# Second layer of a fused two-layer transformer: which unit each projection and turn is issued in

## What is computed

```python
xn = layernorm(x); x = x + linear_attention(xn) + mixture_of_experts(xn)   # layer 0
xn = layernorm(x); x = x + chunked_attention(xn) + gated_ffn(xn)           # layer 1, changed here

# chunked_attention: 16 heads of 8, scale 8 ** -0.5; a query of a 64-token chunk sees
# all keys up to that chunk's end
probs = softmax(q @ k.T * scale)
energy = probs.sum(-1)            # goes through two steps of a small nonlinear recurrence
probs = probs * (0.5 + 0.5 * gate(energy)); probs = probs / (probs.sum(-1) + 1e-8)
out = (probs @ v) @ W_out.T
# gated_ffn: xr, xk are mixes of each token with the one before it
out = sigmoid(xr @ W_r.T) * (relu(xk @ W_k.T) ** 2 @ W_v.T)
```

## Time and profile before

| | |
|---|---|
| median of 3 runs | 1524.6 us (1523.17 to 1528.86) |
| the profiled execution | 1515.43 us |
| its span, first to last instruction | 1513.5 us |
| PE (TensorE matmul) busy | 1404.1 us, 93% |
| DVE (VectorE) busy | 1177.3 us, 78% |
| ACT (ScalarE) busy | 817.2 us, 54% |
| POOL (GpSimd) busy | 523.3 us, 35% |
| mean granted TensorE clock | 0.984 of 2.4 GHz |

### The profile page before, as it was taken

The page is one execution under the profiler, slowest core; times in us unless marked ns, Lnnn a source line. Parts: engine busy times, 40 slices in busy tenths (PEclk is TensorE's granted clock), DMA queues, the critical chain, the costliest instruction groups (busy, mean ns, idle before and its releaser), DMA issues.

```text
span 1513.5 us, 35393 instructions
## 1 busy us (share of the span) xinstructions
PE 1404.1 (93%) x12926; PEld 904.6 (60%) x12926; DVE 1177.3 (78%) x2687; ACT 817.2 (54%) x1562; POOL 523.3 (35%) x942
## 2 busy tenths in 40 slices
PE   5699999999999899999998999999999999999994
PEld 3467677677776799998884444444444444444432
DVE  4789889889888795456677888888888888888752
ACT  2334534544543333334334677777766777776673
POOL 2333234234233111172312244444434444442121
PEclk8999999999999999999999999999999999999997
DMA  4111111111112566776973444333334443332300
GB/s 119 38 42 52 45 48 44 51 47 44 54 33 66 165 208 209 220 245 208 258 195 62 98 106 105 98 98 102 87 93 102 108 103 97 98 92 70 82 9 14
DMA packets 118205, 151.94 MB, mean 100 GB/s; under 512 B 31269, under 2 KB 83109, under 8 KB 113413
## 3 DMA queue, kind: packets, MB, share of 16 engines
q1 hardware_dynamic: 105160, 119.47, 29.0%
q0 software_dynamic: 12880, 30.30, 6.8%
HBM read 108.35 MB, written 40.83 MB: 99 GB/s over the span
## 4 chain that ended last, share of the span: by engine, by line
PE 48%; DVE 32%; POOL 7%; issue 6%; ACT 5%; DMA 1%; SPq 0%; POOLq 0%; DVEq 0%; ACTq 0%
DVE nmax L1516 8%; PE bank L1948 8%; PE bank L1939 8%; DVE P L1205 7%; PE bank L1816 5%; PE bank L1994 5%; PE bank L2017 4%; ACT P L946 3%; PE bank L1773 3%; PE bank L1850 2%; PE bank L1957 2%; PE bank L1864 2%; DVE t L1080 1%; PE bank L2064 1%; DVE t L1078 1%
## 5 line engine op out<-in xcount | busy, mean ns | idle before, releaser
L1516 DVE TENSOR_REDUCE nmax<-bank 128x1 f32<-128x512 f32 (+3 forms) x704 | 428.8, 634 | 84.6 <-PE bank L1994 83.6
L946 ACT ACTIVATE P<-bank 128x512 f32<-128x512 f32 x640 | 371.2, 599 | 183.2 <-PE bank L2017 178.4
L1994 PE MATMUL bank<-KT,QT 76*128 76x512 bf16 (+3 forms) x1024 | 251.3, 303 | 28.5 <-DVE nmax L1516 20.9
L2017 PE MATMUL bank<-QT,KT 78*128 78x512 bf16 (+3 forms) x1024 | 244.5, 301 | 8.9 <-ACT P L946 5.5
L693 POOL DMA_INDIRECT xs_d<-xn,idx x128 | 124.6, 973 | 306.0 <-PE bank L1773 197.9
L1994 PEld LDWEIGHTS bank<-KT,QT 76*128 76x128 bf16 x1024 | 86.8, 97 | 189.1 <-DVE nmax L1516 130.6
L1816 PE MATMUL bank<-P,V 128*32 128x512 f32 (+3 forms) x2048 | 191.3, 447 | 0.0
L1205 DVE TENSOR_TENSOR P<-bank,early_w 128x512 f32<-128x512 f32 x256 | 158.7, 682 | 41.3 <-PE bank L1773 41.2
L910 ACT ACTIVATE hr<-bank 128x512 f32<-128x512 f32 x142 | 84.8, 597 | 175.0 <-PE bank L1939 172.1
L741 POOL DMA_INDIRECT hT<-ys_d,idx x104 | 103.5, 995 | 159.9 <-PE bank L2017 141.8
L2017 PEld LDWEIGHTS bank<-QT,KT 78*128 78x128 bf16 x1024 | 98.6, 98 | 85.0 <-ACT P L946 31.9
(11 more groups left out here) (257 smaller groups left out, 2228.6 us busy)
## 6 DMA issues: line engine op xcount, KB each, us to landing
QT<-parts_d SPq DMA_DIRECT2D x96, 192.0 KB
P<-in_fc SPq DMA_DIRECT2D x71, 256.0 KB, 2.9
P<-in_proj SPq DMA_DIRECT2D x71, 256.0 KB, 3.2
parts_d<-parts SPq DMA_DIRECT2D x32, 384.0 KB, 2.5
P<-xs_d SPq DMA_DIRECT2D x71, 128.0 KB, 3.0
ys_d<-P POOLq DMA_DIRECT2D x71, 128.0 KB, 3.4
KT<-parts_d SPq DMA_DIRECT2D x64, 128.0 KB
KT<-parts_d SPq DMA_DIRECT2D x32, 192.0 KB
```

Of the source, the lines that this page charges most:

```text
L946: nc.scalar.activation(P[s % 2][:, u, :], bank[k % 2][:, :], ACT.Exp, scale=float(DH) ** -0.5).then_inc(s_sb, 1)
L1516: nc.vector.tensor_reduce(nmax[:, s // TWO, h:h + TWO * nh - 1:TWO, j], max_bank(n, k)[:, 0:nh * w].rearrange("p (h w) -> p h w", h=nh), A ...
L1994: ins = pe.matmul(max_bank(n, k)[:, i * w:(i + 1) * w], QT[n.p][0:MROWS, h, j * 128:(j + 1) * 128], KT[n.p][0:MROWS, h, 0:w], start=True, ...
L2017: ins = pe.matmul(bank[k % 2][:, c:c + n], KT[b.p][0:SROWS, h, 128 * kb:128 * kb + 128], QT[b.p][0:SROWS, h, 128 * kb:T], start=True, stop ...
```

## The change

On TensorE these pieces change their unit, nothing else about them changes:

| piece | before | after |
|---|---|---|
| r projection | (0,1) | (0,2) |
| k projection | (0,2) | (0,4) |
| kv projection | (0,6) | (0,8) |
| value projection of the next sequence | (1,1) | (2,8) |
| second q/k projection | (1,5) | (1,6) |
| first turn of oT | (3,3) | (3,2) |
| turn of y | (3,5) | (3,4) |
| output projection | (3,9) | (3,8) |

ScalarE's readers move with them: tanh of r from before the exponential of (0,3) to that of (0,4), the squares of k from (0,4) to (0,6), the eviction of v from (1,2) to (3,0), the eviction of yT from (3,7) to (3,6). VectorE's gate moves from behind maximum 10 to behind 13, the residual from behind 11 to behind 14. The waits on W5 and W6 follow the new order of the pieces in these banks.

```diff
--- before.py
+++ after.py
@@ -1003,15 +1003,15 @@
                 for s in range(SHEETS):
                     for u in range(UNITS):
                         at = (s, u)
-                        if at == (0, 3) and core:
+                        if at == (0, 4) and core:
                             tanh_r(b)
-                        if at == (0, 4) and core:
+                        if at == (0, 6) and core:
                             square_k(b)
                         if at == (0, 7) and core:
                             shift_high(b, 1)
                         if at == (0, 8) and before_:
                             evac_oT(b + -1, 1)
-                        if at == (1, 2) and after:
+                        if at == (3, 0) and after:
                             evac_v2(b + 1)
                         if at == (2, 8) and core:
                             evac_oT(b, 0)
@@ -1031,7 +1031,7 @@
                             tanh_resp(b + -1)
                         if at in ((3, 2), (3, 4)) and after:
                             scale_before(b + 1, u // 2 - 1)
-                        if at == (3, 7) and before_:
+                        if at == (3, 6) and before_:
                             evac_yT(b + -1, False)
                         if core:
                             exp_scores(b, s, u)
@@ -1627,9 +1627,9 @@
 
                     if m == 9 and core:
                         shift_low(b, 1)
-                    if m == 10 and core:
+                    if m == 13 and core:
                         gate_kv(b)
-                    if m == 11 and core:
+                    if m == 14 and core:
                         gate_residual(b)
                     if m in (2, 3, 4, 5) and front and not b.less(L2 + 1):
                         for c in range(2):
@@ -1952,8 +1952,11 @@
             def q_rows(n, c):
 
                 pe.wait_ge(xnT_sb, n.at(1, 1))
-                if c == 0 and within(n + -1):
-                    pe.wait_ge(v2_sb, n.at(1, -L2))
+                if c == 0 and n.less(L2 + 2):
+                    if within(n + -1):
+                        pe.wait_ge(v2_sb, n.at(1, -L2))
+                elif c == 0:
+                    pe.wait_ge(gated, n.at(1, -1 - L2))
                 pe.matmul(qk_bank(n, c)[:, :], wqkv2[:, c, :], xnT[n.p][:, 1:T + 1], start=True, stop=True).then_inc(qk_ps, 1)
 
             def take_part(n, c, k):
@@ -1964,7 +1967,9 @@
                           skip_group_check=True).then_inc((res_part, low_ps)[k], 1)
 
             def v_rows(n):
-                if within(n + -1):
+                if within(n + -1) and within(n + 1):
+                    pe.wait_ge(*split_read(n + 1, 0))
+                elif within(n + -1):
                     pe.wait_ge(gated, n.at(1, -L2))
                 else:
                     pe.wait_ge(*split_read(n, 0))
@@ -2032,9 +2037,7 @@
 
             def project_out2(n):
                 pe.wait_ge(yT_sb, n.at(1, 1))
-                if within(n + 3):
-                    pe.wait_ge(*split_read(n + 3, 0))
-                elif within(n + 2):
+                if within(n + 2):
                     pe.wait_ge(v2_sb, (n + 2).at(1, 1 - L2))
                 elif within(n + 1):
                     pe.wait_ge(gated, (n + 1).at(1, 1 - L2))
@@ -2047,6 +2050,8 @@
             def k_rows(n):
                 if within(n + -2):
                     pe.wait_ge(out_ready, (n + -1).at(1, -L2))
+                elif within(n + -1):
+                    pe.wait_ge(v2_sb, n.at(1, 1 - L2))
                 else:
                     pe.wait_ge(*split_read(n + 1, 0))
                 pe.wait_ge(blended, n.at(2, 2 - 2 * L2))
@@ -2127,33 +2132,33 @@
                             pv(b + -1, SHEETS - 1, u // 2)
                         if u in (1, 3, 5, 7) and s > 0 and core:
                             pv(b, s - 1, u // 2)
-                        if where == (0, 1) and core:
+                        if where == (0, 2) and core:
                             r_rows(b)
-                        if where == (0, 2) and core:
+                        if where == (0, 4) and core:
                             k_rows(b)
                         if where == (0, 5) and core:
                             turn_max(b, 1)
-                        if where == (0, 6) and core:
+                        if where == (0, 8) and core:
                             kv_rows(b)
                         if where == (1, 0) and before_:
                             turn_oT(b + -1, 1, False)
-                        if where == (1, 1) and after:
+                        if where == (2, 8) and after:
                             v_rows(b + 1)
                         if where == (1, 2) and front:
                             turn_xn(b + 2, False)
-                        if where in ((1, 4), (1, 5)) and front:
-                            q_rows(b + 2, u - 4)
+                        if where in ((1, 4), (1, 6)) and front:
+                            q_rows(b + 2, u // 2 - 2)
                         if where in ((1, 8), (2, 0)) and front:
                             take_part(b + 2, s - 1, 0)
                         if where in ((2, 2), (2, 4)) and front:
                             take_part(b + 2, u // 2 - 1, 1)
                         if where == (2, 6) and after:
                             turn_max(b + 1, 0)
-                        if where == (3, 3) and core:
+                        if where == (3, 2) and core:
                             turn_oT(b, 0, False)
-                        if where == (3, 5) and before_:
+                        if where == (3, 4) and before_:
                             turn_y2(b + -1)
-                        if where == (3, 9) and before_:
+                        if where == (3, 8) and before_:
                             project_out2(b + -1)
 
             over_layer2(pe, body2)
```

## The result

The changed kernel took 1508.9 us in the median of 4 runs (1503.41 to 1512.14), the kernel before 1524.3 us beside it on the same chip. The medians lie 15.5 us apart; by the ratio it is 17.5 us (0.0115 of 1524.3), with its interval 13.3 to 21.8. Forecast were 17.6 us, and 1507 us.

A forecast was written before the change was run, and what follows sets the result against it. Neither TensorE nor VectorE bounds the turn; each waits for the other through two score banks. 1.23 us in 13 turns (16.0) plus 1.8 for edge turns, 17.8, gives 1497.6, scaled to 1507 us; range 1501 to 1516.

The forecast's parts named there:

- right: Signs: period about 42.3 us, no VectorE waits before maxima 3, 14 to 16, new 0.6 before 11, L1560 behind GpSimd.
- wrong: Signs: L1560 directly behind a row maximum with E above 14.6 us; VectorE waits again 6.5 us; ScalarE holding TensorE's scores.
- stretch E: Units (2,1) to (3,4): GpSimd's chain sets L1560, added 1.33 us absorbed in some 1.9 us room; gain 0.
- rival (c): (2,8) to (3,2): v is not absorbed; +0.5 us in 14 turns, 7 to 8 us slower, 1532 us; chance 0.14.
- A: Units (0,0) to (0,4): r behind (0,2)'s scores removes VectorE's 0.73 us wait; bounds 0.4 and 0.8.
- B: Units (0,5) to (0,8): kv moved to (0,8) gives new VectorE idle time of 0.64 us before maximum 11; bounds 0, 0.89.
- C: Units (0,9) to (1,4): v leaves (1,1), gates move in, waits ahead of maxima 14 to 16 go; 1.14 us gained.
- The front's sum: Stretches A, B and C together: 0.73 + 1.14 - 0.64 = 1.23 us gained a turn.
- D: Units (1,5) to (2,0): only the second q moves, from (1,5) to (1,6); TensorE sets it, so unchanged.
- F: Units (3,5) to (3,9): VectorE's 0.56 us wait for the output projection moves one place earlier; 0, bound +0.3.
- Rival (a): Idle times only change place through two banks; 0.3 us a turn stays, 4 us, 1520 us; chance 0.18.
- Rival (b): All VectorE waiting outside D and E goes: 2.4 us a turn, 33 us, 1491 us; chance 0.13.

The follow-up runs named there:

- second measurement: The changed kernel run again with no edit, beside the kernel before: 1500.1 us against 1515.1, ratio 0.9885.
- v alone: Kernel before with only the value projection moved from (1,1) to (2,8), with its eviction and waits: ratio 0.9948 to the kernel before, turn 42.90 us.
- v and the gates: Kernel before with the value projection in (2,8), gate and residual behind maxima 13 and 14, r, k, kv unmoved: ratio 0.9977 to the kernel before.
- v twice: Changed kernel with the value projection in (2,8) computed twice into the same bank: ratio 0.9941 to the kernel before, turn 43.13 us.
- the late gather in the kernel before: Kernel before with the expert-row gather put behind the second part of GpSimd's chain: ratio 0.9973 to the unchanged kernel before, turn 43.19 us.
- the best version: Changed kernel with k (0,2), r (0,4), kv (0,6), gate behind maximum 10, residual 13, last sequence's v (1,4): 1494.7 us against 1516.2 before, ratio 0.9859.
- the late gather's trace: Profile of the changed kernel with the expert-row gather put behind the second part of GpSimd's chain: ratio 0.9877 to the kernel before, turn 42.24 us.

## Why the prediction was right

Right in sign and size: 42.3 us forecast a turn, 42.32 measured; 17.6 us forecast, 17.5 measured by the ratio and 15.5 by the medians; in the second measurement 17.4 by the ratio (0.0115 of 1515.1) and 15.0 by the medians. Of the signs that it named, all of "right" were seen. One of "wrong" was seen too: stretch E is 14.70 us long, above the 14.6 given for rival (c). But the other half of that sign, L1560 directly behind a row maximum, was not. E's window ends at TensorE's (3,5), behind the added 1.33 us of work, and F's window is 0.56 us shorter. Step by step:

- **A**: 0.73 us of idle time gained, as said; by starts, maximum 3 comes 0.82 us earlier behind L1576 (3.13 and 2.31 us). The ways in which it might be smaller did not come.
- **B**: new idle time of 0.64 forecast, 0.72 measured, where it was said to be, with TensorE waiting in (0,7).
- **C**: the waits ahead of 14, 15 and 16, 1.14 us, all went, but the reason given, "v leaves (1,1)", carries only part. v alone takes 0.71 us and leaves 0.62 standing ahead of 16. The gates' move was forecast as filling in for idle time; it decides 0.5 us, and only with kv in (0,8), which covers the root that v and the gates alone run into. The prediction had GpSimd in stretch E and never looked at it in C.
- **The front's sum**: 1.23 forecast, 1.51 by the ledger. The term was too small since the idle times were added as the profile lists them. A recorded row maximum lasts 0.69 us, but the next instruction starts 0.60 behind it. Maxima 13, 14 and 15 took 3.20 us to the next start before (1079.29 to 1082.49) and 1.85 after, plus two gates: 1.35 us gained where the gaps listed say 1.14. A's gap and B's new one are each too small in the same way and cancel; the rest is A's combines, which follow closer.
- **D**, costed at nothing: 0.26 us lost between L1550 and L390. VectorE now comes to C's end ahead of TensorE, and TensorE sets D, so that much of the front's gain isn't passed on. This and the previous step cancel, and the 42.3 is closer than the steps were. That is luck in the sum, but the prediction's own times held both sides. On VectorE it had maximum 16 end at 1081.6, where before the next instruction starts at 1083.10: 1.5 us, measured 1.51. On TensorE it had (1,5) at 1082.4 instead of 1083.64: 1.24 us. Measured behind L1576, (1,5) went from 18.55 us (1083.64 - 1065.09) to 17.34 (1088.79 - 1071.45), 1.21. With D set by TensorE, the second is the one that is passed on. The second q moved inside D, but that is not the loss: on TensorE D took 5.13 us before (1083.64 to 1088.77) and 5.14 after.
- **E**: L390 to L1560 was 9.96 and is 9.97. That GpSimd's chain sets it and v is absorbed held, and so the rival (c) fell. The room was overrated: 1.9 us estimated against 1.33 put in leaves 0.57, and v twice shows 0.1. The prediction added up short idle times between TensorE's units as room; the maximum behind L1560 had less, as the late gather in the kernel before shows (0.39 us and it waits).
- **F**: 8.64 and 8.61, nothing, as said.
- **Rival (a)**, that idle time only changes place, describes A and B taken together (0.73 gone, 0.72 new), and in v and the gates without the rest the root's 0.60 for maximum 16's 0.62; it fell because C does not behave like that. **Rival (b)** is not reached by the best version either (41.94 against 41.2).
- By the Trainium skill (Perfetto Trace Analysis, Identifying Performance Opportunities) a repeated gap can mean too little PSUM for the next tile. Had that alone been the cause here, the time would have stayed. With the same banks, order took the turn from 43.58 to 42.32 and then 41.94 us. That more banks would gain too was not tried, so this does not refute it.
- The edge turns were given 1.8 us. By the late gather's trace they gain 2.9 (0.7, 1.5, 0.7), but in the two profiles of the changed kernel itself the slower clock took more than that back (first turn 44.67 and 44.6, last but one 42.78 and 42.77). The timed ratios hold both.

## What to carry to other kernels

When two engines wait for each other through two banks, as TensorE and VectorE do here, take one engine's queue round the whole loop and cut it at fixed instructions: the gap that goes at one place, the gap that comes at the next, and what the third engine then adds are one sum, and a piece's place can be worth 0.5 us with one neighbour and cost 0.3 with another. Test a cover before relying on it by doubling what lies under it: an idle time of 0.54 us ahead of an instruction had room for 0.1 us of work. Measure waits by starts, not by recorded ends.

## What the runs showed of the hardware

- TensorE's granted clock went to its lower level, 1.2 GHz, for 6.8 to 13.7 us about the start of the second layer's first turn, after TensorE had waited for row maxima again and again (0.2 us ahead of each maximum score and 0.66 us at the longest). In three of the fourteen profiles it did so for another 6.8 us about the end of that turn (from 854.6 us in the changed kernel's own), and in five for 6.8 us in the last but one turn, where less work is left. The same code had 13.7 us of it at the start of one execution's first turn and 6.8 in another's. The r projection, 1.16 us in a middle turn, then took 1.91 (TensorE's timeline of the kernel after, start, duration, work):

```profile
809.14 0.39 PE L1999 MATMUL bank<-KT,QT 76*128 76x512 bf16 x1 [0.20 <-DVE nmax L1516]
809.74 0.39 PE L1999 MATMUL bank<-KT,QT 76*128 76x512 bf16 x1 [0.21 <-DVE nmax L1516]
...
815.91 1.91 PE L2069 MATMUL bank<-wrkv,ee 128*128 128x128 f32 x8
```

- A projection of 0.99 us behind float32 value products (v before, 1078.87 to 1079.86) took 0.90 behind bf16 scores (1101.52 to 1102.42). The 0.1 us a piece, counted at nothing, are there, but no run separates them in the time. The neighbours differ in the type of their operands and in their tiles (128*32 and 78*128), and no run tells which of the two it is.
- GpSimd's root (L675, a power of -0.5) of a tile of only 128x4 took 1.05 us, and the five small operations behind it 0.20 us each, 0.27 or 0.28 from start to start (run "v and the gates").
- VectorE's row maximum of 128x512 is recorded at 0.69 us, but the next instruction starts 0.60 us behind its start (1075.00 and 1075.60 in the kernel after).
